# Attention inside a four-block layer: the second step's maxima spread over the half's pieces, value products in pairs, and the last key tiles in all quarters of the buffer

## What is computed

```python
x = x + attn_a(layernorm(x))   # 16 heads of 16, one shared key and value head, causal, biases
x = x + ffn(layernorm(x))      # shared gated unit (1024) plus the best 2 of 8 routed experts (128)
x = x + attn_b(layernorm(x))   # 16 heads of 16 with keys and values of their own, causal, ALiBi
x = x + ffn(layernorm(x))
```

```python
scores = q @ k.T / 4                 # masked: a key after its query counts as -inf
attn = softmax(scores, axis=-1)
out = attn @ v
```

## Time and profile before

| | |
|---|---|
| median of three runs | 1128.58 us (1122.98 to 1128.8) |
| the profiled execution | 1132.09 us, its span 1130.3 us |
| mean granted clock of TensorE | 0.974 |
| TensorE busy | 1027.9 us (91%) |
| VectorE busy | 763.4 us (68%) |
| ScalarE busy | 589.5 us (52%) |
| GpSimd busy | 402.6 us (36%) |
| first attention, first exponential to end of the last step | 55.9 to 312 us |
| second attention | 616.7 to 882 us |

### The profile page before, as it was taken

How to read it: one execution, slowest core, us unless ns; L and a number is a source line. 1 busy time by engine, 2 the same in 40 slices (tenths; PEclk the granted TensorE clock), 3 DMA queues, 4 the chain that set the end, 5 groups by cost and what they waited for, 6 DMA issues and landing times.

```text
span 1130.3 us, 20037 instructions
## 1 busy us (share of the span) xinstructions
PE 1027.9 (91%) x6850; PEld 648.2 (57%) x6850; DVE 763.4 (68%) x1564; ACT 589.5 (52%) x1262; POOL 402.6 (36%) x426
## 2 busy tenths in 40 slices
PE   4889999999999889989899889999999998889997
PEld 3433333333487678878776333334334776788876
DVE  6797888887366854447579778777882668544465
ACT  4445776777743245523255466666776432355332
POOL 3311552323536235254543012321235271352550
PEclk9799999999999999989899899999999999999989
DMA  4712111111034135432169133323301251345341
GB/s 137 182 22 61 38 40 32 29 33 27 25 112 165 52 96 158 113 112 83 38 170 209 28 65 65 62 38 53 70 13 39 84 179 42 96 146 129 116 152 51
DMA packets 66581, 94.99 MB, mean 84 GB/s; under 512 B 19621, under 2 KB 50773, under 8 KB 64423
## 3 DMA queue, kind: packets, MB, share of 16 engines
q1 hardware_dynamic: 48689, 64.33, 22.7%
q0 software_dynamic: 6912, 18.88, 6.5%
q10 hardware_dynamic: 10880, 10.49, 2.7%
HBM read 66.33 MB, written 26.67 MB: 82 GB/s over the span
## 4 chain that ended last, share of the span: by engine, by line
PE 63%; DVE 17%; DMA 6%; issue 4%; ACT 4%; SPq 2%; POOL 1%; another core or an unknown queue 0%; ACTq 0%; DVEq 0%; POOLq 0%
PE o_ps L1014 11%; PE st_ps L996 8%; PE st_ps L225 7%; DVE mab L1612 6%; PE st_ps L227 6%; PE st_ps L226 6%; PE su_ps L957 5%; DMA inverses<-sums 4%; PE su_ps L1154 3%; PE o_ps L1154 3%; PE st_ps L957 3%; PE su_ps L1060 2%; ACT pt L1342 2%; PE st_ps L1187 1%; DVE hf L1825 1%
## 5 line engine op out<-in xcount | busy, mean ns | idle before, releaser
L1342 ACT ACTIVATE pt<-st_ps 128x512 f32<-128x512 f32 (+3 forms) x768 | 329.9, 493 | 191.7 <-PE st_ps L996 112.1
L996 PE MATMUL st_ps<-qs,ks 99*128 99x512 bf16 (+7 forms) x768 | 245.7, 333 | 11.5 <-ACT pt L1342 5.5
L1612 DVE TENSOR_REDUCE mab<-su_ps 128x1 f32<-128x512 f32 (+3 forms) x302 | 189.3, 659 | 19.7 <-PE su_ps L961 14.6
L721 POOL TENSOR_SCALAR_AFFINE_SELECT pt<-pt 128x512 f32<-128x512 f32 x112 | 71.4, 638 | 347.5 <-ACT pt L1342 347.5
L957 PE MATMUL su_ps<-ks,qs 102*128 102x512 bf16 (+7 forms) x538 | 162.9, 331 | 9.9 <-DVE mab L1612 9.2
L1014 PE MATMUL o_ps<-pt,vp 128*32 128x512 f32 (+3 forms) x1536 | 166.0, 506 | 1.9 <-POOL pt L721 1.0
L996 PEld LDWEIGHTS st_ps<-qs,ks 99*128 99x128 bf16 (+1 forms) x768 | 74.1, 99 | 114.1 <-ACT pt L1342 59.9
L802 POOL DMA_INDIRECT rows_in<-rows,source x80 | 77.7, 972 | 131.1 <-DVE source L1870 60.3
L1366 ACT CAST hh<-hf 128x512 fp32r<-128x512 f32 x64 | 39.7, 620 | 146.6 <-DVE hf L1825 138.7
L225 PE MATMUL st_ps<-xt_h,wu 128*128 128x512 f32 x256 | 103.4, 404 | 6.9 <-DVE xt_l L1504 4.1
L1612 DVE TENSOR_REDUCE mab<-st_ps 128x1 f32<-128x512 f32 (+2 forms) x152 | 100.2, 659 | 13.2 <-PE st_ps L961 9.5
(11 more groups left out here) (230 smaller groups left out, 2033.6 us busy)
## 6 DMA issues: line engine op xcount, KB each, us to landing
wu_raw<-w_units_dram SPq DMA_DIRECT2D x32, 384.0 KB
outs<-rows_out ACTq DMA_DIRECT2D x40, 256.0 KB
q_parts<-hml SPq DMA_DIRECT2D x16, 384.0 KB, 3.3
wexp_raw<-w_units_dram SPq DMA_DIRECT2D x16, 384.0 KB, 7.2
qs<-q_parts SPq DMA_DIRECT2D x14, 384.0 KB
inv<-inverses SPq DMA_DIRECT2D x128, 32.0 KB, 1.8
rows<-xn SPq DMA_DIRECT2D x8, 512.0 KB, 6.6
qs<-q_parts SPq DMA_DIRECT2D x14, 256.0 KB
```

Source lines behind the costliest of these rows:

```text
L721: pool.affine_select(block, block, [[0, 4], [1, P]], ALU.is_ge, 0.0, base=0, channel_multiplier=-1).then_inc(masked, 1)
L996: last = pe.matmul(bank[KM_BANKS[n % len(KM_BANKS)]][:, lo - CH * part:hi - CH * part], key_stack(l, s)(j)[0:rows, P * kt:P * kt + P], que ...
L1342: act.activation(pt[:, kt % 2, j, lo:hi], bank[KM_BANKS[i % len(KM_BANKS)]][:, lo - CH * part:hi - CH * part], ACT.Exp, scale=1 / np.sqrt( ...
L1612: dve.tensor_reduce(to, bank[SU_BANKS[n % len(SU_BANKS)]][:, 0:share * width].rearrange("p (j k) -> p j k", j=share), AX.X, ALU.max).then_ ...
```

## The change

Six things change, all in the attentions.

- The score units of step 1: in the first attention eight still stand behind piece 15, in the second eight now stand behind pieces 9 to 15. The others are spread from piece 16 to 98% of the step, so that the transposition comes behind piece 46. Of step 2's first eight units two follow there and six behind piece 47. From step 1 on the lists are the same as before.
- The products of steps 1 to 7 are made for two blocks at a time, behind piece 1 of each odd block (blocks q-3 and q-2). Step 0's last two are made ahead of step 1's first piece.
- In steps 1 to 7 blocks 8 to 11 lie in the four quarters in turn, so that an exponential waits for the product four blocks back.
- The copy of the early output half comes behind block 9 (piece 39) in steps 1 to 7.
- The stacks of steps 3 to 7 are loaded from ScalarE's queue, group by group behind pieces 1, 9 and 17 of step s-2 (in the second attention 3, 2 and 2 DMAs, in the first one each).
- Stack 2 of the second attention is loaded after the second half's maxima are sent. (In the first attention its place is unchanged.)

```diff
+LOAD_BEHIND = [1, 9, 17]
+def quarter(s, q):
+    kt, part = quads(s)[q]
+    if s and kt >= HALF:
+        return divmod(kt - HALF, 2)
+    return kt % 2, part
 def last_quad(S, q):
-    kt, part = quads(S % STEPS)[q]
-    own, former = ([n for n, (k, a) in enumerate(quads(t % STEPS)) if a == part and k % 2 == kt % 2] for t in (S, S - 1))
+    own, former = ([n for n in range(NQ) if quarter(t % STEPS, n) == quarter(S % STEPS, q)] for t in (S, S - 1))
...
-    behind[SECOND_AT[l]] += [(1, 0), (0, NSU - 1)] + [(1, u) for u in range(1, 1 + AHEAD[l])]
-    n = SECOND_AT[l] + 1
+    behind[SECOND_AT[l]] += [(1, 0), (0, NSU - 1)]
+    for i in range(AHEAD[l]):
+        behind[SECOND_AT[l] + (HALF_PIECES - SECOND_AT[l]) * i // AHEAD[l]].append((1, 1 + i))
+    n = HALF_PIECES
     for u in range(1 + AHEAD[l], NSU):
-        t = at[SECOND_AT[l]] + (1 - lead - at[SECOND_AT[l]]) * (u - AHEAD[l]) / (NSU - 1 - AHEAD[l])
+        t = at[SECOND_AT[l]] + (SECOND_BY - at[SECOND_AT[l]]) * (u - AHEAD[l]) / (NSU - 1 - AHEAD[l])
...
         for u, t in enumerate(s - 1 - lead + through):
-            while at[n] < t - 1e-9:
+            while at[n] < t - 1e-9 or u > 1 and n < PIECES - 1:
                 n += 1
-AHEAD = (8, 0)
+SECOND_BY = 0.98
+AHEAD = (8, 8)
...
+        def exponentials(s, q, lo, hi):
+            own, at = quarter(s, q)
+            first = CH * (at - quads(s)[q][1])
+            return pt[:, own, :, first + lo:first + hi]
...
@@ SP @@
             def load_stack(l, s):
-                if s >= SBANKS:
-                    sp.wait_ge(st_ready, PIECES * (step_no(l, s - SBANKS) + 1))
...
                     send_parts(l, 3)
-                    load_stack(l, 2)
...
                 send_half(l, 1)
+                if l:
+                    load_stack(l, 2)
                 for s in range(STEPS):
                     S = step_no(l, s)
-                    if 1 <= s < STEPS - 2:
-                        load_stack(l, s + 2)
...
@@ TensorE @@
-                    if n == HALF_PIECES:
-                        for early in range(HALF - PV_LAG, HALF):
+                    if n in (HALF_PIECES, PIECES):
+                        for early in range(n // 4 - PV_LAG, n // 4):
                             values(l, 0, early)
                     key_major(l, s, q, j)
-                    if j == PV_BEHIND and n // 4 >= PV_LAG and n // 4 - PV_LAG not in range(HALF - PV_LAG, HALF):
+                    if j == PV_BEHIND and s == 0 and q >= PV_LAG and q not in range(HALF, HALF + PV_LAG):
+                        values(l, 0, q - PV_LAG)
+                    if j == PV_BEHIND and s and q % 2 and n // 4 > NQ + 1:
+                        values(l, *divmod(n // 4 - PV_LAG - 1, NQ))
                         values(l, *divmod(n // 4 - PV_LAG, NQ))
...
@@ ScalarE @@
+            def load_stack(l, s, group):
+                b, g = divmod(s, G)
+                r = s % SBANKS
+                heads = slice(4 * g, 4 * g + 4)
+                if group == 0:
+                    act.wait_ge(st_ready, PIECES * (step_no(l, s - SBANKS) + 1))
+                rows, parts = query_group(l, b, heads, group)
+                act.dma_start(qs[rows, r, :, :], parts).then_inc(stk_in[r], 16)
+                if l:
+                    rows, parts = key_group(l, b, heads, group)
+                    act.dma_start(ks[rows, r, :, :], parts).then_inc(stk_in[r], 16)
+                if l and group == 0:
+                    act.dma_start(qs[ROWS:ROWS + ALIBI, r, :, :].bitcast(U16),
+                                  slopes[:, 4 * g:4 * g + 4, :]).then_inc(stk_in[r], 16)
...
-                        act.activation(pt[:, kt % 2, j, lo:hi], bank[KM_BANKS[i % len(KM_BANKS)]][:, lo - CH * part:hi - CH * part], ACT.Exp,
+                        act.activation(exponentials(s, q, lo, hi)[:, j, :], bank[KM_BANKS[i % len(KM_BANKS)]][:, lo - CH * part:hi - CH * part], ACT.Exp,
                                        scale=1 / np.sqrt(D)).then_inc(p_ready, 1)
+                        if 1 <= s < STEPS - 2 and n in LOAD_BEHIND:
+                            load_stack(l, s + 2, LOAD_BEHIND.index(n))
                         if s and n == 4 * PV_LAG - 1:
                             take_output(S - 1, 1)
-                        if n == 4 * (last_of(s, 0) + PV_LAG + 1) - 1:
+                        if n == 4 * (last_of(s, 0) + PV_LAG + 1 + (s > 0)) - 1:
                             take_output(S, 0)
```

More of the change, by code:

```diff
@@ L511, in load_stack @@
                 b, g = divmod(s, G)
-                r = s % SBANKS
                 heads = slice(4 * g, 4 * g + 4)
-                if s >= SBANKS:
-                    sp.wait_ge(st_ready, PIECES * (step_no(l, s - SBANKS) + 1))
                 for group in range(len(GROUPS)):
                     rows, parts = query_group(l, b, heads, group)
-                    sp.dma_start(qs[rows, r, :, :], parts).then_inc(stk_in[r], 16)
+                    sp.dma_start(qs[rows, s, :, :], parts).then_inc(stk_in[s], 16)
                     if l:
                         rows, parts = key_group(l, b, heads, group)
-                        sp.dma_start(ks[rows, r, :, :], parts).then_inc(stk_in[r], 16)
+                        sp.dma_start(ks[rows, s, :, :], parts).then_inc(stk_in[s], 16)
                 if l:
-                    sp.dma_start(qs[ROWS:ROWS + ALIBI, r, :, :].bitcast(U16),
-                                 slopes[:, 4 * g:4 * g + 4, :]).then_inc(stk_in[r], 16)
+                    sp.dma_start(qs[ROWS:ROWS + ALIBI, s, :, :].bitcast(U16),
+                                 slopes[:, 4 * g:4 * g + 4, :]).then_inc(stk_in[s], 16)
             def load_key_rows():
@@ L718, in mask_exponentials @@
                         if masks_after(l, s):
-                            block = pt[:, kt % 2, :, lo:lo + P]
+                            block = exponentials(s, q, lo, lo + P)
                             pool.wait_ge(p_ready, PIECES * S + 4 * q + 4)
@@ L1014, in values @@
                     last = pe.matmul(o_ps[32 * j:32 * j + 32, lo:hi], vp[:, QT * b + kt, 4 * g + j if l else 4 * (g % 2), :],
-                                     pt[:, kt % 2, j, lo:hi], start=kt == 0,
+                                     exponentials(s, q, lo, hi)[:, j, :], start=kt == 0,
                                      stop=kt == (QT if part else HALF) - 1)
```

## The result

The changed kernel takes 1135.66 us (median of 8 runs, 1131.47 to 1140.59), the kernel before beside it 1127.03 (8 runs): a ratio of 1.0079, 95% interval 1.005 to 1.0108. It is 0.8% slower, where 1105 us was forecast. The profiled execution took 1140.59 us, 8.5 more than the one of before.

The account below looks back on a forecast made before the run. TensorE was taken to set the steady step's pace (busy 29.44 of 29.74 us). Terms -12.8 + 3 - 7 - 0.6 + 0 - 6.5 = -23.9 us, taken from the median 1128.58, gave 1105 us; range 1088 to 1119.

Parts of the forecast that it names:

- steps 1 to 5 (-12.8 + 3 - 7): Both attentions: -12.8 us from moved stack loads, +3 for ScalarE issuing them, -7 from pairs, quarters and late copy.
- the 0.3 us a step for starving by pairs: Steps with paired products: a pair holds TensorE 2.0 us, so VectorE starves longer, costing 0.3 us a step.
- the 0 for step 7: Last step of each attention: a copy 2 us later eats the gain of pairs and quarters, 0 (-2 to +2).
- the -0.3 for each step 6: Step 6 of each attention: the maxima bind more without units behind its end; -0.3 us each, -0.6 in all.
- The 0.24 us per entry: TensorE, steps 1 to 7: entering a product costs 0.10 us, leaving 0.15; each pair saves 0.24, at most 20 in all.
- The late copy in a steady step: From the product at piece 37 to the next step: 7.2 us for 6.8, maxima last by 0.6 to 1.3.
- Loads: Stack loads off SP's queue in steps 1 to 5: 11.8 us gained in the second attention, 0.94 in the first.
- The price of ScalarE's issues: ScalarE issuing 50 load DMAs: 0.5 us a step in the second attention, 0.1 in the first; +3 (0 to 10).
- The rival by which the loads still hold the inverses: Loads slow the inverses through the shared 16 engines even from another queue; the 11.8 us stay, 1117 us; chance 0.12.
- Quarters: Last key tiles of a step: ScalarE's 3.2 us wait for products goes; TensorE gains 0.7 us a step.
- First steps: Start of each attention, maxima spread and two products moved ahead: -2.5 us in the first, -4 in the second, together -6.5.
- the fourth rival: Each step's first key piece waits for maxima behind the late copy on SP, clock may halve: 1146 us; chance 0.08.

Follow-up runs that it names:

- single products: Changed kernel with one product at a time, two blocks behind, and the early copy back behind block 8: 1081.72 against 1107.08 us for the kernel before, 0.9773.
- the kernel without the spreading: Kernel before plus loads on ScalarE's queue and four quarters, one product at a time, score units at their old places: 0.9796 against the kernel before.
- the best version: Changed kernel with one product at a time, two blocks behind, and early copy: 0.9773 against the kernel before; with maxima also sent ahead of the gathering, 0.9766.

## Why the prediction was wrong

Forecast and measured, in us, over both attentions. The measured column is worked out from the two profiled executions, from the exponentials' starts and, for the projections, from the start of their first matmul.

```
                                    forecast   measured
step 0                                 -6.5       -4.5
steps 1 to 5 (-12.8 + 3 - 7)          -16.8       -0.4
step 6                                 -0.6       +4.0
step 7 and the projections' wait        0         +7.1
outside the attentions                  0         +2.3
sum                                   -23.9       +8.5
```

The terms that failed are, in the order of their size, the 0.3 us a step for starving by pairs, the 0 for step 7, and the -0.3 for each step 6.

*Pairs: the saving right, the starving wrong.* The 0.24 us per entry held to the hundredth. The starving was put at 0.3 us a step from VectorE's banks alone, and "twenty-five of VectorE's 29.7 us are used" was taken as room. It measured 1.95 (2.85 less 0.90 against single products), 0.71 of it between key pieces, at ScalarE's banks, where spare time had been counted as cover. The forecast had split a step at the product behind piece 37. Ahead of it 1.1 us were to be gained; in the steady step 0.4 were lost (22.96 us from the first exponential, 22.53 before). That is 1.5 us a step, and over ten steps 15 of the 16 us that steps 1 to 5 missed by. Against single products with the same quarters a pair costs 0.6 a step rather than saving 1.1.

*The late copy in a steady step: right, its landing time included.* The prediction gave 7.2 us from the pair at piece 37 to the next step, for 6.8 before. It took 7.1 (250.81 to 257.90). The copy ended 3.3 us after the pair's start, and the wait for the maxima was there, both as forecast. It costs 0.7 us against an early copy, as the forecast's 0.6 to 1.3 had it.

*The late copy elsewhere: wrong.* What the forecast gave away was the slack, 1.9 us of it before, and it priced only the mean transfer. In three of the twelve steps the third maxima transfer landed 2.9 to 3.5 us after its issue and not 1.9, and now each of these went into the step: +1.4 us from the product of piece 37 to the next step's first exponential in the first attention's step 4, +2.2 in the second's step 1, +2.3 in the second's step 6. In step 6 a second thing came on top. The timeline of its end in the second attention:

```profile
849.47 0.59 ACT L1363 COPY ou<-o_ps 128x512 f32<-128x512 f32 x1
850.09 0.60 SPq L587 DMA_DIRECT2D sums<-ou  x1
850.73 0.47 SPq L664 DMA_DIRECT2D wu_raw<-w_units_dram  x1
851.25 1.83 SPq L582 DMA_DIRECT2D qs<-nmx  x3
...
855.84 2.39 PE L1010 MATMUL st_ps<-qs,ks 105*128 105x512 bf16 x5 [2.79 <-DMA qs<-nmx]
```

A load of weights stands between the gathering and the maxima, in both kernels; the list of what the copy delays on SP left it out. TensorE stood 2.8 us, and then ran 6.8 us at the lower clock. Step 6 took 30.38 and 31.85 us for the 28.8 of the forecast. Behind step 0 the changed kernel ran 17.0 us at the lower clock in the two attentions, the kernel before 6.8, and the one with the copy behind block 8 none.

*Step 7: wrong.* "A copy 2 us later eats the step's pairs and quarters: 0". The wait of the projections grew by 3.1 and 1.8 us, and step 7 itself became longer by 1.4 and 0.8.

*Loads: right, and the price too.* The steps of the second attention that the forecast counted gave 11.6 us for its 11.8, and step 4 gave 0.8 besides. The price of ScalarE's issues was put at 0.5 us a step in the second attention. Beside single products nothing of it is seen (29.16 us in both attentions). Beside pairs it is there: with the copy behind block 8 a steady step takes 30.27 us in the second attention and 29.78 in the first, and in the changed kernel 31.0 and 30.48. The exponentials fall behind right after the issues behind pieces 1 and 17. The 0.94 of the first attention did not come; it has another cause (below).

The rival by which the loads still hold the inverses did not come true, but its mechanism is real. The Trainium skill, DMA: Bandwidth & Descriptors, under Issuing engines are not separate DMA queues, says that DMAs of different issuing engines run on the same 16 DMA engines, and that a second issuing engine saves only the time of issuing. The trace agrees with the first half: spreads that met loads on the other queue took 4.7 to 8.0 us and not 1.6 to 2.9. The second half does not cover the 12.4 us that steps 1 to 5 of the second attention gained: they came from what no longer stands behind the loads in SP's list.

*Quarters: right.* 0.7 us a step forecast; alone they gave 0.6 in a steady step, 1.2 in step 6 and 1.4 in step 7, 9.8 us in all. Their gain in a steady step lies behind piece 37: with single products it is 6.6 us from there to the next step's first exponential, and 7.2 without the quarters. In the changed kernel the late maxima set that stretch, at 7.5.

*First steps: right alone by luck, counted twice in the sum.* 6.5 us were forecast, 2.5 in the first attention and 4 in the second. Alone the spreading gave 7.8, nothing of it in the first attention, where step 1 gave back what step 0 gained, and 6.5 in the second, which come also from the loads. With both, 1.3 us are left (the kernel without the spreading against the best version, inside the error).

The outcome lies nearest the fourth rival, at a chance of 0.08: the maxima at each step's start, by SP's order and the late copy. Its condition (over 2 us more than the 0.4 charged, at twelve boundaries) was met at none; the largest was 2.3 us over before. The slower time came from pairs and copy together, which the rivals had kept apart. The forecast treated as independent three things that hang on one another: pairs, the copy that must follow their product, and SP's list behind the copy.

## What to carry to other kernels

When work is bunched to save switches, compare it with what the buffers between engines can even out, in pieces and not in mean busy time: three banks cover a piece or two, and 15% or 28% of spare time on the other engines covers nothing if it falls in the wrong block. When an instruction moves, read every in-order queue behind it to its end, and let what the next stage waits for stand ahead of what only the stage after it needs. Slack in front of a transfer is not free to spend: it covers the few that land late. And add up gains only where they remove different waits.

## What was not expected of the hardware

- An entry into the products' tiling with the way out costs 0.24 us whether the products are of 512 or of 128 columns. In a steady step with single products a product's first matmul starts 0.10 us, and the matmul behind it 0.14 to 0.15 us, later than the columns at 2.4 GHz account for, in all twelve products.
- Small transfers on SP's queue took longer when they met loads on ScalarE's. Of the 32 KB spreads in steps 1 to 5 of the second attention, with the loads alone moved, those that met loads took 4.7 to 8.0 us and those that met none 1.6 to 2.9. The 8 KB inverses met none (1.4 to 2.9 us); behind the same loads on one queue they took 9.2.
- Behind step 0, an 8 KB transfer of the maxima lands 1.9 us after its issue in most steps, and 2.6 to 3.5 us after it in a few steps of nearly every execution. What it meets there stays open.
- The excess of about 1.1 us in step 3 of the first attention and step 4 of the second has nothing to do with the loads. The first is GpSimd's. In the kernel before, it works on weights (`split_weights`) when the mask of the step's first block is due, and the product of that block starts only behind the mask (the profile puts the wait down to a copy, which had ended at 169.54):

```profile
166.12 3.44 POOL L773 TENSOR_TENSOR wp_l<-wraw,wp_h 128x1536 fp32r<-128x1536 f32 x1
169.53 0.63 POOL L721 TENSOR_SCALAR_AFFINE_SELECT pt<-pt 128x512 f32<-128x512 f32 x1
...
170.26 1.06 PE L1014 MATMUL o_ps<-pt,vp 128*32 128x512 f32 x8 [0.87 <-ACT ou L1330]
```

  With products later (pairs, or three blocks behind) that step is no longer than its neighbours, or by 0.2 us. The second step is the one in which TensorE adds the masks itself: 32 matmuls of 128 columns, 1.7 us at 2.4 GHz (an estimate from the columns).
